# A macaron block on one core: the banks for expert results and for the preparation of attention change, and the written order of the work with them

## The reference

```python
x = x + 0.5 * ffn(layernorm(x))      # mixture of 8 experts, the best 2 of each token
x = x + attn(layernorm(x))           # 16 heads, each token sees itself and the 8 before it
x = x + 0.5 * ffn(layernorm(x))      # the same experts again
# ffn:  scores = softmax(xt @ Wg + bg); top 2 of 8; out = sum_k prob_k * (gelu(xt @ W1[e] + b1[e]) @ W2[e] + b2[e])
# attn: scores = q . k_window / 0.56, softmax over a window of 9, weighted sum of v, @ Wo
```

## Time and profile before

| | |
|---|---|
| median of 3 runs | 1211.37 us (1206.4 to 1219.11) |
| the profiled execution | 1195.72 us, span of its records 1193.9 us |
| TensorE busy | 919.0 us, 77% |
| VectorE busy | 644.4 us, 54% |
| GpSimd busy | 669.9 us, 56% |
| ScalarE busy | 500.2 us, 42% |

### The profile page before, as it was taken

The page is one execution under the profiler, slowest core; times in us unless marked ns, Lnnn a source line. Parts: engine busy times, 40 slices in busy tenths (PEclk is TensorE's granted clock), DMA queues, the critical chain, the costliest instruction groups (busy, mean ns, idle before and its releaser), DMA issues.

```text
span 1193.9 us, 22506 instructions
## 1 busy us (share of the span) xinstructions
PE 919.0 (77%) x6345; PEld 762.5 (64%) x6345; DVE 644.4 (54%) x1309; ACT 500.2 (42%) x1215; POOL 669.9 (56%) x593
## 2 busy tenths in 40 slices
PE   3446868567897798988898838998988868865984
PEld 3334747456775587777777725677766756754874
DVE  6655133423147587898979998687851511110222
ACT  4433524334534273655644415634434433322432
POOL 2475445446387766455668556356765555555452
PEclk9999769889898799999999978989985988897997
DMA  8813212252113421026112121223222223432683
GB/s 274 235 55 73 55 44 50 65 137 67 42 58 62 134 54 41 19 59 139 33 39 55 23 96 55 45 52 68 50 60 53 51 59 84 116 97 69 154 190 120
DMA packets 170344, 96.44 MB, mean 81 GB/s; under 512 B 137696, under 2 KB 154390, under 8 KB 169332
## 3 DMA queue, kind: packets, MB, share of 16 engines
q1 hardware_dynamic: 152276, 59.29, 21.9%
q0 software_dynamic: 17952, 35.71, 9.5%
HBM read 25.77 MB, written 52.35 MB: 65 GB/s over the span
## 4 chain that ended last, share of the span: by engine, by line
PE 41%; issue 16%; DMA 10%; POOL 9%; another core or an unknown queue 8%; DVE 6%; SPq 6%; ACT 3%; ACTq 0%; POOLq 0%; DVEq 0%
PE bank L966 18%; PE bank L949 12%; POOL x_sorted L579 7%; DMA x_sorted<-hl,slots_all 5%; PE bank L854 3%; DMA x_sb<-in_L_attn_x 2%; PE bank L960 2%; ACT h_f L756 1%; POOL y_pairs L596 1%; SPq L476 1%; PE bank L840 1%; PE bank L867 1%; SPq L466 1%; SPq L452 1%
## 5 line engine op out<-in xcount | busy, mean ns | idle before, releaser
L596 POOL DMA_INDIRECT y_pairs<-y_sb,tile_ids x305 | 359.5, 1179 | 330.0 <-issue 215.9
L756 ACT ACTIVATE h_f<-bank,b_cols 128x256 f32<-128x256 f32 (+1 forms) x736 | 264.1, 439 | 443.3 <-PE bank L949 298.3
L579 POOL DMA_INDIRECT x_sorted<-hl,slots_all x256 | 301.9, 1179 | 179.4 <-issue 86.8
L966 PE MATMUL bank<-w_sb,h_f 128*128 x2440 | 355.2, 299 | 22.6 <-issue 15.3
L966 PEld LDWEIGHTS bank<-w_sb,h_f 128*128 128x128 f32 x2440 | 315.3, 206 | 45.1 <-issue 28.2
L949 PE MATMUL bank<-xsT,w_hl 128*128 128x256 f16 (+1 forms) x2208 | 263.3, 270 | 56.6 <-issue 20.9
L949 PEld LDWEIGHTS bank<-xsT,w_hl 128*128 x2208 | 201.2, 104 | 93.8 <-issue 66.7
L1412 DVE TENSOR_TENSOR y_sb<-bank,tile_ids 128x256 f32<-128x256 f32 (+1 forms) x184 | 68.8, 375 | 342.2 <-PE bank L966 169.0
L960 PE MATMUL bank<-b_hl,ones_b 64*128 x184 | 49.5, 269 | 72.8 <-DVE y_sb L1412 59.8
L960 PEld LDWEIGHTS bank<-b_hl,ones_b 64*128 64x128 f16 x184 | 17.1, 93 | 113.2 <-issue 110.6
L1197 DVE TENSOR_TENSOR prod<-score,qkv 128x2304 f32<-128x2304 f32 x32 | 81.6, 2550 | 0.2
(11 more groups left out here) (159 smaller groups left out, 851.3 us busy)
## 6 DMA issues: line engine op xcount, KB each, us to landing
y_in<-y_pairs SPq DMA_DIRECT2D x28, 512.0 KB
x_sorted<-no_rows SPq DMA_DIRECT2D x7, 720.0 KB
y_pairs<-y_sb,tile_ids POOLq DMA_INDIRECT x305
x_sb<-in_L_attn_x SPq DMA_DIRECT2D x4, 1024.0 KB, 5.7
x_sorted<-hl,slots_all POOLq DMA_INDIRECT x256
x_sorted<-no_rows SPq DMA_DIRECT2D x56, 72.0 KB
out<-x_sb SPq DMA_DIRECT2D x3, 1024.0 KB
xsT<-x_sorted SPq DMA_TRANSPOSE x184
```

Source lines behind the costliest of these rows:

```text
L579: pool.indirect_dma_start(out=x_sorted[p], out_offset=bass.IndirectOffsetOnAxis(ap=slots_all[:, at:at + 1], axis=0), in_=hl[:, c % 2, i // ...
L596: pool.indirect_dma_start(out=y_pairs, out_offset=bass.IndirectOffsetOnAxis(ap=tile_ids[:, t.n % IDS, i, 0:1].bitcast(U32), axis=0), in_=y ...
L756: ins = act.activation(h_part(t, b)[:, k, :], bank[h_banks.uses[u][0]][:, k * t.slots:(k + 1) * t.slots], ACT.Gelu, bias=b1_cols[:, bass.d ...
L966: ins = pe.matmul(into[:, half, :], h_part(t, c // t.per)[:, c % t.per, half * P:(half + 1) * P], w2_flat[:, bass.ds((e * HC + c) * D, D)] ...
```

## The change

Two lines of code change, and the five order strings with them. In stage 1 the results get banks 3 and 4 in turn. The preparation keeps bank 2 alone. The strings are new throughout: TensorE's and ScalarE's each have 48 letters more, since a step of products is one matmul and one copy now.

```diff
-        h_banks, y_banks = Banks((0, 1, 2), (0, 1), (0, 1, 2, 6)), Banks((3, 7), (3,), (3, 7))
+        h_banks, y_banks = Banks((0, 1, 2), (0, 1), (0, 1, 2, 6)), Banks((3, 7), (3, 4), (3, 7))
...
-        prep_bank = [bank[2], bank[4]]
+        prep_bank = [bank[2]]
         PREPS = len(prep_bank)
...
 POOL_ORDER = (
-    "sssssyysyysyyyyyyyyyyyyyysyyyyyysyyyyyyyyyysyyyyyyyyysysysyyyyysyyyyyyyyyysyyysyyyyyyyyyyyyyssssssssyyyyyyyyyy"
+    "sssssyysyyyyyyyyysyyyyyysyyyyyyysyyyyyyyyyysyyyyyyyyyyysyyssyyysyyyyyyyyyyysysyyyyyyyyyyyyyyyyssssssyyyyyysyyy"
...
```

More of the change, by code:

```diff
@@ L72 @@
-    "aapaappaaapppaappaapppppppppaaaepapraaaeeaeeeeepeeereeeeeeereeeeeeerererererereeeeeeereeaaaeeaeeeeeeeeeeeeeeea"
-    "eeeeeeeeaeeeaeaaaeeeeeeaaeaaeaaaeeeaaeaaeaaaeeeeeaaeaaeeeeeeeeerererrerereererereeeeeereeeeeeeeeeeeeeeeeeeeeee"
+    "rrrrrrrrrrrrrrrrrrerrrrrrrrreeeeeeeeeeereerrreeeeereeeeeeeeeeeeeeeeeeeeeeeeeeeeeeeeeeeeeerrrreeeeeeereeeeeeeee"
+    "eeeeeeeeeeeeeeeeeeeeeeeeeeeeeeeeeeeeeeeeeeeeeeeeeeeeeeeeeeepeepeepepeepepeepeepeepepeepeepeepeepeepeeepeepeepe"
+    "epeepeapapapapapapaapppppeepeeeeeeeeeeeeeeeeeeeeeeeaaaeepepeeeeepeeeeepeeepeeepepeeaeeeeeeeeaeeaapeeaaaeeepeee"
@@ new lines @@
+    "paapaapepaapapepaapaapapapapeapaepaapeepeapapapaaaeeaaeeeeeprereerpereererererereeaaapeepeeeeaeeeeeeeeeeeeaaar"
+    "eeeeeeeeeeeeeaaaepepepeepepeppaapapaepaapapepaapaapepapapapeepaaepaaepepeapapeapapreapaaaeeeeeeeeeeeeeeeeepeep"
+    "eepeepeeeaeaarrrarrrrraaarpppppapapapppppppppepaaaaaaappaapaapaaappaapaapppaappaapraaarerearerereereerereeeeee"
+    "eeereeeeeeaeaeepapeeeeeeeeeeeeeeeeeeeeeeeeeaeeeeeeeeeeeeaeaaeeeaaaeeeeeeeaaeaaeaaaeeeeeaaeaaeaaaeeeeaaeaaeeeee"
+    "eeeeeeeeeerrererrrrrreeeeeeereeeeeeeeeeeeeeeeeeeeeeeeeeeeeeeeeeeeeeeeeeeeeeeeeeeeeeeeeeeeeeeeeeeeeeeeeeeeeeeee"
@@ L84 @@
+    "aaeaaaearraaraaaehhaaaeaeaeaeaaeaaraearaaeaeaappreearerapphpphpeeaaeaaeaaahhaaaaaaaaahhaaaaaaarrareaaeaahaaaee"
+    "aeaeaeaeaeeaeaeahaeeaaaaapprarapprpprprrhhrarararrahhraaaaaaaaaahhaaaaaaaaaarraraaaaahhaaaaeaarererarrrhhrerer"
+    "errareaeaeaeaeaaeaeaeaeaaaaaaeaaaeaahaaaaaeaaeaaaaehhhaarrerehhrrereerrrrhrhrerrereeeeeeeeeeeeephhepeeppeeepep"
+    "eepepeehheeeeeeeeeeeeeeeeeeeppeeeppeeeeeeeeeeeeeepppp"
 )
 ACT_ORDER = (
-    "rrrrrhrrhrrrrrrrrrrrrrrrrrehrrrrhrrrrrrrrhrheeeeeerreeereerreereereeerheeheerreeeeerrrheeeeeereeeeeeeeeeeeheee"
@@ new lines @@
+    "eeeeeeeeeheeeeeeeeeeeeppeppeppeppeppeppeppepeeppephepepepepepeepepepepepppphppppppahppeepeeeeeeeeeheeeeppppeee"
+    "ppeheppeeppeeppppeeepeeaaaeepeeeeppaappeppppaapppppepaappepeeppprrrhrrhrrreearepreerprererererepepeeeeeeeaaaer"
+    "eeeeeeeeppppppppeppppppphapaepepeepppaapphppppepaaepppepperprrhprrrprrreeaeeeeeeepepepepehrrrrrrraaarppppppppp"
+    "ppppppppppphpppepaapphpaappppaapppppprrrrrrrrrphhrerererarereereeeeereeeeppeeeeeeeeeeeeeeeeeeaaaeeeeeeheeaaeee"
+    "eaaeheeaaeeeeerrrrrrrrrheereererrrrhrreeeeeeeeeeeeeeeeeeeeeeeeeheeeeeeeeeeeeeeeeeeeeeeeeeeeheeeeeeeeeeeeeeeeee"
@@ L92 @@
+    "eeeeeeeeeeeeeeeeeeeeeeeeeeeeeeeeeeeeeeeeee"
 )
 POOL_ORDER = (
-    "sssssyysyysyyyyyyyyyyyyyysyyyyyysyyyyyyyyyysyyyyyyyyysysysyyyyysyyyyyyyyyysyyysyyyyyyyyyyyyyssssssssyyyyyyyyyy"
-    "yyyyyyyyyyssssssssyyyyyyyysyysyyyysyyyssssyyyyyysyyyyyysyyyyyyyyyyysssyyyyyyyyyyyysyyyyyysssyyyyyyyyyyyyyyyyyy"
+    "sssssyysyyyyyyyyysyyyyyysyyyyyyysyyyyyyyyyyysyyyyyyyyyyysyyssyyysyyyyyyyyyysysyyyyyyyyyyyyyyyyssssssyyyyyysyyy"
+    "yyysyyyyyyssssssssyyysyyyyyyyyyyyyssyysyssssyyyyyyysyyyyyyyyyyyyyyyssyyyyyyyyysyyyyyyyyyssssyyyyyyyyyyyyyyyyyy"
@@ L98 @@
 SP_ORDER = (
-    "tttttttttttttttttttttttttttttyyttttyytttttttttttttttttttttttyytttyyttttttttttttttttttyyttttyytttttttttttttttyy"
-    "yytttttttttttttttttttttttttttttttttttttttttttttttttttttyytttyytttyttttttttttttyytttyytttyyytttyytttytttttyyyyy"
+    "tttttttttttttttttttttttttttttyyttttyyttttttttttttttttyyttttyyttttttttttttttttttttttttttyyttttyytttttttttttttyy"
+    "yytttttttttttttttttttttttttttttttttttttttttyyttttytyttttyyytttyytttytttttttttttttttttttyytttyyttttttttttyyyyyy"
     "yyy"
```

21 lines of the change are left out of this document (4 added, 17 removed).

## The result

The changed kernel takes 1223.87 us (median of 4 runs, 1217.66 to 1234.83) against 1208.88 us for the kernel before beside it (4 runs, 1205.74 to 1219.11): a ratio of 1.015, with a 95% interval of 1.010 to 1.020. It is slower by 1.5%, where 1.2% faster was forecast. A second comparison on another chip gave 1.017 (1.011 to 1.023). The profiled execution takes 1222.58 us.

What follows compares the result with a forecast made beforehand. No engine is full; whichever ends last in each stage bounds it, and TensorE's longest wait is for the result bank. Terms -15 + 4 - 5 + 0 + 2 + 0 = -14 us, so 1211.4 - 14 = 1197 us, range 1176 to 1216.

Steps and rivals of the forecast that it cites:

- The second result bank: TensorE's waits for VectorE's take of results, parts 1 to 6: shorter waits give -15 us, ends 0 and -40.
- the 25 us named: Sign of the second result bank: TensorE's wait for the take falls from 59.8 us to below 25.
- One preparation bank: Preparation steps directly following another wait for copies, 0.74 us each: +4 us, ends 0 and +16.
- the 10 to 20 named: Sign of one preparation bank: waits for product copies grow from 3.5 to 10 to 20 us, mostly between parts 3 and 4.
- my end of +16: High end of one preparation bank: 22 of 128 preparation steps follow directly on another, 16.3 us.
- Part 0: Reordered part 0: VectorE's 22.9 us wait for group 2's rank goes, -5 us, ends 0 and -16.
- The end of part 1: Channel sums behind the tiles, GpSimd's last 16 group 2 scatters later: 0 us, ends -7 and +7.
- Route 5: Behind tile 3.23: more VectorE steps before slots, shorter GpSimd wait to first scatter: +2 us, ends -6 and +19.
- rival 2: Route 5 starts late at VectorE's group 3 combine, first scatter at 709: +19 us, whole about 1224 us, chance 0.14.
- GpSimd's bursts: Row scatter bursts for parts 5 and 6 cut differently, same number: 0 us, ends -8 and +8.
- the 212 named as the sign of the bank: Sign in part 4: it lasts 212 us or less instead of 224.
- Rival 1: Waits only move: TensorE waits for gelu or rows instead of the bank; about -4 us, 1207 us, chance 0.30.
- Rival 3: More than summed: TensorE's clock stays up where it fell, bank gives 30; about -37 us, 1174 us, chance 0.08.

Runs made afterwards that it cites:

- e5: Changed kernel's order, preparation alternating banks 2 and 4, results in bank 3 alone up to tile 4.9, then banks 3 and 4; 1.0446 against the kernel before.
- e6: Changed kernel, but results in bank 3 alone up to tile 4.9 and banks 3 and 4 after, preparation in bank 2 alone; 1.0467 against the kernel before.
- e3: Kernel before in its own order with both bank changes, product pairs split into single steps, a few steps placed later; 1.0502 against the kernel before.
- the second pair: Traces of the changed kernel and the kernel before, both unchanged, on one other chip; the changed kernel's ratio there is 1.0168.
- e8: Kernel before with results in banks 3 and 4 from tile 4.10 on, and part 0 in the new order on every engine; 0.9947 against the kernel before.
- e7: Kernel before in its own order, with results in banks 3 and 4 only from tile 4.10 on; 0.9983 against the kernel before.
- e13: Changed kernel once more, unchanged, on another chip; 1.0168 against the kernel before.
- e12: Changed kernel up to about tile 4.9, old order behind it with the old cut of GpSimd's bursts; 1.024 against the kernel before.
- e1: Changed kernel with route 5 back beside the tiles of part 3 on TensorE, ScalarE and VectorE; 1.0156 against the kernel before.
- e2: Changed kernel with only VectorE's order altered: route 5 and its gates ahead of group 3's combine and statistics; 1.0146 against the kernel before.
- e9: Changed kernel with VectorE's route 5 ahead of the combine, and three tiles of part 4 ahead of most of attention 3; 1.0302 against the kernel before.
- e10: Changed kernel with only the first three tiles of part 4 put further ahead on TensorE, ScalarE and VectorE; 1.0397 against the kernel before.
- e11: Changed kernel with VectorE's route 5 ahead of the combine and 7.1 us of VectorE's window sums left out, output differing; 1.0179 against the kernel before.
- e15: Changed kernel with VectorE's route 5 early, preparation in banks 2 and 4, results in bank 3 alone up to tile 4.9; 1.037 against the kernel before.
- e17: The edits of e11 and e15 together on the changed kernel; one profile alone, stretch ahead of part 4 103.9 us.
- e18: e12 once more, on another chip; 1.0225 against the kernel before.

## Why the prediction was wrong, step by step

**The second result bank, -15.** Its mechanism held: the wait fell below the 25 us named, to 10.2. Its size can't be told without the order. In the order of the change the bank is worth 23 to 38 us, toward the upper end of -40, and 16 to 21 of these lie in part 3, where I had taken 2 for parts 2 and 3 together. In the order of before it is worth 0 to 2 us. In parts 4 and 5, where I had taken -10, the changed kernel loses 4.5 us instead. Of the 28 us less that TensorE waits for takes there, 16.5 came back as waits for gelu (25.3 us instead of 8.8) and 4.5 as starts that wait for nothing that the profile shows; where the rest went isn't shown. This is the second step that failed. I worked the term out from waits of the old order and added it to an order that was not the old one.

**One preparation bank, +4.** In the new order 2.5 us (e5 to e6), with one result bank. Products stand at two lines, and I had counted the waits of one. TensorE's waits for their copies at the other, before and after:

```profile
PE bank L837 <- ACT qkv L685: 1.6, 1, 1.6
```

```profile
PE bank L839 <- ACT qkv L687: 7.1, 8, 2.8
```

Together they grew from 5.1 to 24.2 us, above the 10 to 20 named, and only 6.6 of them lie between parts 3 and 4, where most was to be. The term also put at nothing that products one at a time keep TensorE busy for longer: products and turned pairs take 95.7 us of the run instead of 80.9, and 88.3 in e5, where they are single but have two banks. In the old order one bank costs 58 us. That isn't a breach of my end of +16, which stood for 22 adjacent steps: for the 61 of e3 the same 0.74 us gives 45. Measured, it is 0.95 us a step. What the rule leaves out is a step that finds ScalarE at another task: in e3 it waits up to 10.8 us, and TensorE, which passes nothing, holds the tiles behind it.

**Part 0, -5.** Right in size: part 1 begins at 225.0 instead of 231.0, and 10 us sooner in the second pair. In the changed kernel parts 1 and 2 took it back (+2.3 and +4.9); in the old order 4 us of it are left at the end (e8 to e7), with overlapping intervals.

**The end of part 1, 0.** +2.3 us, in the range.

**Route 5, +2.** This is the step that failed first and cost most: I took the work ordered behind tile 3.23 to make part 3 shorter and to fit into the free time behind it. The stretch from the take of 3.23 to the up of 4.0 is 22.8 us longer. I had the case in rival 2, with a first scatter at 709 (it came at 711.6) and +19, and gave it a chance of 0.14, on one condition: that tile 3.23 is not taken sooner than 662. I held a sooner take for likely because 12 us of TensorE's work had gone behind that tile. It was taken at 680.1. The work did leave part 3, but part 3 did not get shorter. Parts 2 and 3 before and after, TensorE by line (columns: count, busy, mean ns, idle before):

```profile
L840 PE MATMUL bank<-wqkv,xnT_p 128*128 128x384 f32 x64 | 23.6, 494 | 0.1
L960 PE MATMUL bank<-b_hl,ones_b 64*128 x48 | 12.5, 261 | 19.1 <-DVE y_sb L1412 12.5 <-issue 6.3
L837 PE MATMUL bank<-wqkv,xnT_p 128*128 128x256 f32 x32 | 8.3, 381 | 0.0
```

```profile
L842 PE MATMUL bank<-wqkv,xnT_p 128*128 128x384 f32 x66 | 28.1, 509 | 5.2 <-ACT qkv L687 5.2
L962 PE MATMUL bank<-b_hl,ones_b 64*128 x48 | 12.7, 265 | 1.7 <-DVE y_sb L1414 1.7
L839 PE MATMUL bank<-wqkv,xnT_p 128*128 128x256 f32 x32 | 10.7, 419 | 2.8 <-ACT qkv L687 2.8
```

TensorE is the fullest engine there, and its busy time did not fall: 275.4 us instead of 275.0. The logits, turned rows and rank of route 5 that moved out took 7.0 us with them, and the products, one at a time now, took 6.9 us more. The 17.4 us less of idle time at the result bank came back at products (7.9), ups, downs, turned pairs and window sums. VectorE has 16.3 us less to do in these parts, but it is the less full of the two, and waited instead: 31.5 us for results in part 2 instead of 17.1, and 29.6 instead of 14.8 in the second pair.

What stands behind tile 3.23 is settled by the written order. VectorE is busy 90.1 us in that stretch in the changed kernel and in e13, instead of 72.0 and 72.1, and TensorE 70 us instead of 54. It is the same in e12, on whose chip VectorE has none of the waits that the profile marks `remote`, their source being unknown:

```profile
596.20:701.60 105.40, 68.44 (x272) 47.41 (x272) 89.97 (x173) 36.16 (x83) 52.36 (x36) 0.74 0.16 50
```

So the longer stretch doesn't come from what was late in part 2. The order put 18 us of VectorE's work and 16 of TensorE's, attention 2 and route 5, behind the last tile, and I priced 8.7 us of it, less 7.5, on VectorE, and TensorE's at nothing.

That rival 2 names 1224 us, the measured median, is in part luck. Its place is right, but route 5 is not all of it: the stretch is 98.0 us in e1, with route 5 out of it, and 82.8 in the kernel before. Part 3, the stretch and part 4 last 461 us together before, 485 in the changed kernel, 492 in e1 with the logits ahead and 486 in e2 with route 5 ahead; e9 and e10 moved tiles, and part 4 paid for it; e11, e15 and e17 took work and waits from the stretch, and it stayed within 2 us, behind a wait that their order had made longer. None of the late steps tried here holds part 4 alone. e1 is the one run in which both chains start early (scatters 2.4, the combine 13.3, the normalised rows 27.8 us behind the take). It gives back 7.5 of the 23 us, less what part 3 paid for it. VectorE is still busy 84.6 us there and TensorE 61.5, against 72.0 and 54.2 before. That the other 15 us are attention 2's is read from this; no run put attention 2 back, and it stays open.

**GpSimd's bursts, 0.** In the range as far as e12 and e18 tell, where the whole old order from tile 4.9 on, with the old cut, gave nothing back.

**The sum.** By stages -6.0 + 2.3 + 4.9 - 0.8 + 22.8 + 2.0 + 2.5 - 0.8 = +26.9 us between the two profiled executions, of which the one of before lies some 13 us under the median beside it; the medians differ by 15. Between the forecast -14 and this lie 41 us: 21 of route 5's stretch, 14.5 of the bank in parts 4 and 5, and most of the rest in parts 1 to 3. Parts 4 and 5 last 341 us, and part 4 226 instead of the 212 named as the sign of the bank. Rival 1's mechanism is there too: VectorE's place as the one waited for was in part taken by gelu. **Rival 3** has nothing for it: the mean granted clock fell from 0.898 to 0.863, and from 0.897 to 0.883 in the second pair. Its rows were also thin ground: TensorE is busy 88% at 0.50 in the earlier trace rows and 90% at 0.96 in the earlier trace rows, so the busy share alone doesn't tell the two levels apart.

A second result buffer that costs no preparation bank would be the upper half of bank 3, since a result fills 256 of 512 columns. It wasn't tried: the Trainium skill (PSUM — Partial Sum Buffer, PSUM bank collisions raise a hardware error) says that TensorE and VectorE must not be at one bank at once, and no run here shows it.

## What to carry to other kernels

A written order and the buffers that it was written for have one price together. The same bank was worth 23 to 38 us in one order and next to nothing in the other, and the other bank some 2 us and 58; a term worked out from the waits of one order can't be added to another, and two runs with orders and buffers crossed show it at once. A price per step carries over better than a sum: count the steps that follow directly on another in the order that will run. Cutting a step in two has a price of its own on the engine, besides the waits. When an order takes work out of a stage, don't take the stage to be shorter: add up what the fullest engine does there before and after. Here its busy time stayed the same, so the stage did, and the work was met again behind it. When a step is brought forward on an engine, look what it pushes back: if that feeds the same end by another way, nothing is won. And a kernel that carries a second edit is no stand-in for the one that is missing from the comparison.
